# Pair products of levels 5 and 6 copied by ScalarE in partition blocks, in a pre-norm delta-rule attention with a mixture of experts

## The reference

```python
def step(S, inp):                       # attention, for each head, S is 128 x 128
    qt, kt, vt, gt, bt = inp
    S = S * jnp.exp(gt)[..., None]
    err = jnp.einsum('bhk,bhkv->bhv', kt, S)
    delta = bt[..., None] * (vt - err)
    S = S + kt[..., None] * delta[:, :, None, :]
    ot = jnp.einsum('bhk,bhkv->bhv', qt, S)
    return (S, ot)
...
x = x + attention(layernorm(x))         # q, k, v from projections, a short convolution and silu
x = x + mixture_of_experts(layernorm(x))
```

## Time and profile before

| | |
|---|---|
| median of 3 runs | 6114.02 us (6113.93 to 6114.86) |
| the profiled execution | 6113.91 us, its span 6112.2 us |
| TensorE busy | 5880.2 us, 96% of the span |
| VectorE busy | 4405.0 us, 72% |
| ScalarE busy | 3050.1 us, 50% |
| GpSimd busy | 1867.6 us, 31% |

### The profile page before, as it was taken

How to read it: one execution, slowest core, us unless ns; L and a number is a source line. 1 busy time by engine, 2 the same in 40 slices (tenths; PEclk the granted TensorE clock), 3 DMA queues, 4 the chain that set the end, 5 groups by cost and what they waited for, 6 DMA issues and landing times. The chain is left out here.

```text
span 6112.2 us, 92718 instructions
## 1 busy us (share of the span) xinstructions
PE 5880.2 (96%) x33208; PEld 4262.8 (70%) x33208; DVE 4405.0 (72%) x7563; ACT 3050.1 (50%) x5133; POOL 1867.6 (31%) x1636
## 2 busy tenths in 40 slices
PE   5699999999999999999999999999999999899999
PEld 2377777777777777777777777777777777644444
DVE  7688888888888888888888888888888888411110
ACT  2355555555555555555555555555555555301101
POOL 2233333333333333333333333333333333100000
PEclk8899999999999999999999999999999999899999
DMA  2101111101011111101011111110111111221221
GB/s 76 40 27 35 28 35 29 35 27 32 27 35 29 35 29 29 35 27 31 28 35 29 35 28 35 28 33 25 35 28 35 29 28 29 69 106 62 80 78 47
DMA packets 183711, 236.04 MB, mean 39 GB/s; under 512 B 25048, under 2 KB 128088, under 8 KB 179168
## 3 DMA queue, kind: packets, MB, share of 16 engines
q1 hardware_dynamic: 111072, 188.22, 10.3%
q10 hardware_dynamic: 72192, 41.95, 2.3%
HBM read 183.75 MB, written 46.38 MB: 38 GB/s over the span
## 5 line engine op out<-in xcount | busy, mean ns | idle before, releaser
L632 PE MATMUL bank<-xT,weights 128*128 128x512 f32 x4096 | 2156.8, 614 | 36.1 <-DMA bg_col<-in_L_attn_bg 36.1
L1264 POOL TENSOR_TENSOR KR<-KR,decay_u 128x256 f32<-128x256 f32 x896 | 972.5, 1085 | 3050.1 <-PE bank L658 3050.1
L896 DVE SCALAR_TENSOR_TENSOR conv<-pre,taps,conv 128x512 f32<-128x512 f32 x1152 | 1139.6, 998 | 24.7 <-ACT conv L1104 15.5
L658 PEld LDWEIGHTS bank<-KQ,KR 128*128 128x128 f32 x7168 | 905.9, 191 | 188.5 <-issue 181.4
L911 DVE TENSOR_TENSOR KQ<-KQ,decay_u 128x512 f32<-128x512 f32 x896 | 641.1, 716 | 496.9 <-PE bank L658 496.4
L658 PE MATMUL bank<-KQ,KR 128*128 128x128 f32 x7168 | 962.7, 277 | 4.3 <-DVE KQ L911 3.2
L931 DVE COPY_PREDICATED all_pairs<-level_mask,bank 128x512 f32<-128x512 int32 x896 | 799.9, 893 | 0.0
L632 PEld LDWEIGHTS bank<-xT,weights 128*128 128x128 f32 x4096 | 662.5, 192 | 190.2 <-issue 130.8
L1149 ACT ACTIVATE T_inv<-bank 128x256 fp32r<-128x256 f32 x640 | 249.8, 390 | 949.9 <-PE bank L700 949.9
L681 PEld LDWEIGHTS bank<-T_inv,pairs 128*128 128x128 f32 x3072 | 464.1, 192 | 365.7 <-issue 332.0
L681 PE MATMUL bank<-T_inv,pairs 128*128 128x64 f32 x3072 | 712.7, 357 | 0.7 <-DVE T_inv L947 0.5
(11 more groups left out here) (160 smaller groups left out, 8704.7 us busy)
## 6 DMA issues: line engine op xcount, KB each, us to landing
decay_u<-decay_scratch SPq DMA_DIRECT2D x128, 510.0 KB
beta_u<-beta_scratch SPq DMA_DIRECT2D x128, 256.0 KB
y_scratch<-y_rn ACTq DMA_DIRECT2D x128, 256.0 KB, 2.3
y_in<-y_scratch SPq DMA_DIRECT2D x32, 1024.0 KB, 4.8
xt<-in_L_attn_hidden_states SPq DMA_DIRECT2D x8, 1024.0 KB, 5.4
x_in<-in_L_attn_hidden_states SPq DMA_DIRECT2D x32, 256.0 KB, 5.1
out<-o_out ACTq DMA_DIRECT2D x32, 256.0 KB, 2.0
w<-in_L_ffn_W SPq DMA_DIRECT2D x8, 704.0 KB, 5.0
```

The lines of the kernel that those rows point to most:

```text
L632: last = nc.tensor.matmul(bank[w % 2][:], weights[par][:, w, k, :], xT[:, k, u % J * UC:(u % J + 1) * UC], start=k == 0, stop=k == KC - 1)
L658: last = nc.tensor.matmul(to[:, :, i], KR[:, cols(i)], halves(KQ[:, :, cols(i)], l, 1), start=True, stop=True)
L896: nc.vector.scalar_tensor_tensor(conv[:, w], pre[:, w, :, t:t + P], taps[par][:, w, t:t + 1], conv[:, w], ALU.mult, ALU.add).then_inc(step ...
L1264: nc.gpsimd.tensor_tensor(first_halves, first_halves, second.to_broadcast([P, UC >> (l + 1), 1 << l]), ALU.mult).then_inc(keys_scaled.sem, 1)
```

## The change

The copies of levels 5 and 6 leave VectorE. ScalarE makes them in a new function, `keep_upper_pairs`, without masks: the rows that count are whole blocks of partitions (at level 5 partitions 0 to 31 and 64 to 95, at level 6 partitions 0 to 63), and for each block one copy goes to `all_pairs` and one to `pairs`. That is four ACTIVATE instructions at level 5 (two of 32 x 256, two of 32 x 128) and two at level 6 (64 x 512 and 64 x 256). The new signal `upper_pairs_ready` carries them: `transpose_keys` waits for its first count, `keep_all_pairs` for the second, and TensorE's `level(0)` of the next step for the second of the unit before. On ScalarE's queue level 5 stands between `inverse_norm(0)` and `first_tap(0)`, and level 6 between `keep_scaled` and `keep_rows`.

```diff
--- before.py
+++ after.py
@@ -479,7 +479,8 @@
     hats_ready = signal("hats_ready", 1)
     unit_ready = signal("unit_ready", 1)
     scaled = signal("scaled", LEVELS)
-    pairs_ready = signal("pairs_ready", LEVELS + 1)
+    pairs_ready = signal("pairs_ready", LEVELS - 1)
+    upper_pairs_ready = signal("upper_pairs_ready", 2)
     t1_ready = signal("t1_ready", 1)
     x1_ready = signal("x1_ready", 1)
     zi_ready = signal("zi_ready", LEVELS - 1)
@@ -649,6 +650,8 @@
                     return
                 if l == 0:
                     wait(pe, unit_ready, m, 1)
+                    if b is not None:
+                        wait(pe, upper_pairs_ready, b, 2)
                 else:
                     wait(pe, scaled, m, l)
                     wait(pe, keys_scaled, m, l)
@@ -799,7 +802,7 @@
                 if m is None:
                     return
                 wait(pe, keys_scaled, m, LEVELS)
-                wait(pe, pairs_ready, m, LEVELS)
+                wait(pe, upper_pairs_ready, m, 1)
                 for i in range(B):
                     last = nc.tensor.transpose(bank[4][:, cols(i)], KR[:, cols(i)], ident[:])
                 last.then_inc(k_transposed.sem, 1)
@@ -1059,10 +1062,8 @@
             convolve(2, (1, 2))
             add_identity_to_z(6)
             scale(5)
-            keep_pairs(5)
             convolve(2, (3,))
             scale(LEVELS - 1)
-            keep_pairs(LEVELS - 1)
             hats()
             take_residual(b, 0)
             keep_chunk_decay()
@@ -1176,6 +1177,25 @@
                 wait(act, yg_ready, c, 1)
                 nc.scalar.activation(y_sq[:], yg[:], ACT.Square).then_inc(y_sq_ready.sem, 1)
 
+            def keep_upper_pairs(l):
+
+                if m is None:
+                    return
+                wait(act, level_done, m, l + 1)
+                if b is not None:
+                    wait(act, z_done, b, l)
+                    wait(act, pairs_kept, b, 1)
+                wait(act, pairs_ready, m, LEVELS - 1)
+                size = 1 << l
+                src = bank[3 + l % 2][:].rearrange("p (k b m s) -> p k b m s", k=2, b=B, s=size)
+                both = all_pairs[:].rearrange("p k (b m two s) -> p k b m two s", b=B, two=2, s=size)
+                keys = pairs[:, l].rearrange("p (b m two s) -> p b m two s", b=B, two=2, s=size)
+                for i in range(P // (2 * size)):
+                    rows = slice(2 * size * i, 2 * size * i + size)
+                    nc.scalar.activation(both[rows, :, :, i, 1], src[rows, :, :, i], ACT.Copy)
+                    last = nc.scalar.activation(keys[rows, :, i, 1], src[rows, 0, :, i], ACT.Copy)
+                last.then_inc(upper_pairs_ready.sem, 1)
+
             def keep_scaled():
                 if m is None:
                     return
@@ -1193,7 +1213,8 @@
             def keep_all_pairs():
                 if m is None:
                     return
-                wait(act, pairs_ready, m, LEVELS + 1)
+                wait(act, pairs_ready, m, LEVELS - 1)
+                wait(act, upper_pairs_ready, m, 2)
                 nc.scalar.activation(pairs_scan[m % 2][:], all_pairs[:], ACT.Copy).then_inc(pairs_kept.sem, 1)
 
             def inverse_rms():
@@ -1237,9 +1258,11 @@
             nc.scalar.preload_act_table_set("natural_log_exp_and_others")
             take_delta()
             inverse_norm(0)
+            keep_upper_pairs(5)
             first_tap(0)
             inverse_norm(1)
             keep_scaled()
+            keep_upper_pairs(6)
             keep_rows()
             inverse_rms()
             keep_all_pairs()
```

## The result

| | before | changed |
|---|---|---|
| median | 6114.44 us (6113.93 to 6115.08, 4 runs) | 6159.90 us (6158.78 to 6163.15, 4 runs) |
| ratio, 95% interval | | 1.0076 (1.0064 to 1.0088) |
| span of the profiled execution | 6112.2 us | 6157.0 us |
| VectorE busy | 4405.0 us | 4154.3 us |
| ScalarE busy | 3050.1 us | 3280.4 us |

The account below looks back on a forecast made before the run. TensorE was taken as the bound, busy 985 of 1000 us. To the profiled 6113.9 us came 0 for the removal, 0 for level 5, about 0.5 for the first two boundaries and 0.1 for the median: 6114.5 us, range 6110 to 6145.

Parts of the forecast that it names:

- The removal: VectorE loses two L931 and two L939 copies, 2.64 us a step, 338 us in all; gain nothing.
- C: Rival: less loaded VectorE starts its run before level 5's `ZI` earlier, shortening L700's 75.4 us; half gives 6076 us; chance 0.07.
- Level 6's copies: On ScalarE behind `keep_scaled`: 0.78 us more, covered by the 1.81 us ScalarE idles at `take_t(1)`.
- The slack of `T_inv`: At TensorE's weight load L681: 0.37 us of lateness are free, more than the 0.31 expected, so TensorE loses nothing.
- `transpose_keys` and L1027: Other users of moved work, both covered: 0.43 us spare at the first; `keep_scaled` ends by 3017.51, L1027 starts at 3018.77.
- Signs that missed: Signs of being right in the profile after: VectorE busy down about 338 us, ScalarE up about 300.
- The signs of being wrong: In the profile after: third copy or tap starting only after its forerunner's end, or a step longer than 39.46 us, among others.
- the overlap of the copies at level 5: On ScalarE, independent instructions were taken to overlap by 0.10 us each.
- the list of users of the moved work: Waiters on ScalarE's moved work: `hats` to `T_inv`, `transpose_keys`, `keep_scaled` with L1027, `take_t(1)`, `level(0)`; each taken as covered.
- level 5's time: Four ScalarE copies ahead of the first tap add 0.96 us; loss per step starts at 1.02 us.
- rival A: ScalarE copies starting on another partition don't overlap: level 5 takes 1.22 us, costing 26 us, 6140 us; chance 0.22.
- A few tenths: In the last steps, without projections, a few tenths of a us could go either way.

Follow-up runs that it names:

- e2: Changed kernel with level 5's copies back on VectorE, only level 6 copied by ScalarE: 6114.92 us, ratio 1.0003.
- e3: Changed kernel with `y_sums` on TensorE one place later, behind project(1, (2,)): 6146.85 us, ratio 1.0054.
- e4: Changed kernel with the second block's level-5 copies reading and writing partitions 0 to 31, that block's products left out: 6122.96 us, ratio 1.0013.
- e7: Changed kernel with the second block's level-5 copies reading PSUM at partition 64 but writing SBUF at 0, products of that block left out: 6142.22 us.
- e8: Changed kernel with the second block's level-5 copies reading PSUM at partition 0 but writing SBUF at 64, products of that block left out: 6137.77 us.
- b1_order: Kernel before, with `add_identity_to_z(5)` ahead of two calls and a tap of v's convolution behind `add_identity_to_z(6)`: 6003.61 us, ratio 0.9817.
- e1: Changed kernel with ScalarE's level-5 copies moved ahead of `take_projection(0)`, where ScalarE idles: 6118.71 us, ratio 1.0005.

## Why the prediction was wrong

**What held.** The removal gained nothing: the time freed on VectorE went into its two waits, and C, the faster case, had nothing to it; L703 waited 75.2 us, as L700 had 75.4. Level 6's copies and everything behind them on ScalarE were covered (e2). The slack of `T_inv`, 0.37 us, was right: e3 lost 0.20 us at L684 and 0.22 over the step, for a lateness of some 0.59. `transpose_keys` and L1027 were not late in the step read.

**Signs that missed.** VectorE's busy time fell by 250.7 us and not 338, ScalarE's rose by 230.3 and not 300. The prediction added up the durations of instructions that overlap, and took L931's mean over all levels, 0.893 us, where in the step read the two that go last 0.73 and 0.74. So what was freed is 1.96 us of busy time a unit and not 2.64. It had no part in the loss. The signs of being wrong did speak: the third copy and the tap began only behind their forerunners' ends, and the step was over 39.46 us.

**Two terms failed.** The loss needs the first of them, the overlap of the copies at level 5: without the holds nothing is lost, with both waits in place (e4). With the holds and `T_inv`'s wait alone it is 0.22 us a step (e3), and the waiter that the list left out makes it 0.33.

**The step that failed: the list of users of the moved work.** The prediction followed the second norm only along `hats` to `T_inv`. The norm's Ln has a second user, by way of the bank: `y_sums` writes bank 2 and waits for `sums_taken`. That wait had 0.25 us to spare, less than `T_inv`'s 0.37, so it decides: the loss starts at a level-5 time of 0.65 + 0.25 = 0.90 us and not at 1.02. The prediction's own value of 0.96 would already have cost 0.06 us a step.

**The mis-sized term: level 5's time.** The prediction had 0.96 + 0.61 us from the first copy to the Ln; it was 1.09 + 0.75. It counted 0.10 of overlap at every copy, the tap and the norm. Short copies were cheaper than extrapolated: 367 and 252 ns against 390 and 289, together 0.12 us less. But three overlaps were lost, at the third copy, the tap and the Ln, 0.39 us together against e4, 0.13 each. That is rival A. It had been given 0.22 and two of the three places; the third, the Ln, was missed, because the last read of PSUM, not the neighbour in the queue, is what counts. The sum by parts: 0.84 + 0.61 us without holds (e4) would be 0.19 late and free; 0.39 us of holds make it 0.58 (0.59 against TensorE), and the loss 0.34, measured 0.33 and 39.9 us over the steady part. With rival A's mechanism and its own slack the prediction came to 26 us.

The rule of the Trainium skill behind that rival ("VectorE: DVE Perf Modes", section Two Vector instructions with no wait between them) keeps, for each memory, where the last read and the last write started, and holds an instruction that differs. It is written for VectorE. In e4, e7 and e8 ScalarE follows it at all nine places where it was looked at, with starts at partitions 0 and 64 only. By the Trainium skill, "ScalarE: Activation LUTs", section What ACT_TABLE_LOAD costs, a 128 would take 293 ns (an estimate from its 186 ns + 0.833 ns a column); that was high for these copies from PSUM, 252 ns.

**The last steps.** "A few tenths" was wrong too: the profiled execution of the changed kernel took 9.0 us more there. Ten microseconds, in the columns of the earlier trace rows, soon after the last projections and 30 us behind the last projection copy: before, changed, and b1_order, which hasn't the change:

```profile
5260.00:5270.00 10.00, 9.92 (x64) 7.62 (x62) 3.45 (x10) 3.51 (x8) 0.00 (x0) 0.98 0.01 2
```
```profile
5297.00:5307.00 10.00, 10.00 (x31) 6.90 (x31) 1.50 (x3) 1.15 (x3) 0.00 (x0) 0.50 0.00 0
```
```profile
5144.30:5154.30 10.00, 10.00 (x37) 7.93 (x36) 1.11 (x2) 1.53 (x4) 0.00 (x0) 0.50 0.01 2
```

TensorE is granted 1.2 GHz in a stretch where it had nearly 2.4 before, and does 31 matmuls in place of 64. In the ten microseconds ahead of it the two traces agree: 8.98 us busy at a granted 0.85. b1_order has the low clock there too, and its last steps take 80.1 us. In the eleven profiled executions that part takes from 73.4 us (before) to 87.7 (e4, whose step is unchanged), and the kernel before alone ran from 6109.88 to 6122.35 us in 25 executions. So it isn't shown that the change costs anything in the last steps, and some 5 of the 45 us stay unexplained; what decides when the clock falls was not tried and stays open. The steady loss doesn't hang on it: from the first to the last projection copy the profiled executions take 5007.2 us before, 5047.1 changed, 5007.9 in e1, 5007.2 in e2, 5033.6 in e3 and 5006.5 in e4.

## What to carry to other kernels

Moving work to a less busy engine is paid by that engine's tightest deadline, not by its mean load: list every waiter on each signal behind the insertion point, bank reuse included, and take the smallest slack. Look for an idle gap ahead of that deadline (e1: the same copies, four calls earlier, cost nothing). And before unloading an engine on which the bound engine waits, see whether the wait is one of order: here one call moved ahead of two others (and a tap behind another) brought 1.8%, and the unloading nothing.

## What the runs showed of the hardware

- ScalarE holds an instruction back when its input starts at partition 64 and the last read of that memory at 0, or the other way round, and the same for its output and the last write: 0.11 to 0.14 us later each, the overlap of 0.10 and a gap of 0.02 to 0.03. From the first copy to the Ln it takes 1.45 us with no hold (e4), 1.70 and 1.71 with two (e7, e8), 1.84 with three (changed). Other starts than 0 and 64 were not tried. With one start, the next instruction follows a 32x256 copy after 0.26 us and a 32x128 copy after 0.16 (e4).
- The number of partitions doesn't change a copy's time much: 64x512 from PSUM took 577 ns, 64x256 365 and 32x256 367, against 592 and 390 for 128 partitions.
- The profile's wait before a matmul can be too short: the stall at L700 showed as 0.66 us a step and gave back 0.93, the difference that the distance between the weight loads shows (1.72 against 0.78).
